# The residual moves into the output projection's sum on TensorE, and ScalarE copies the sum out

## The reference, cut to what matters

```
xn  = layernorm(groupnorm(x)) * ln_w + ln_b          # over 384 channels, per token
xb, z = split(xn @ in_proj_w.T)                       # 768 channels each
xc  = silu(conv1d(xb, 4 taps) + conv_b)
dt, B, C = split(xc @ x_proj_w.T);  dt = softplus(dt @ dt_w.T + dt_b)
h[t] = exp(dt[t] * A) * h[t-1] + dt[t] * xc[t] * B[t] # 768 channels x 16 states
y[t] = sum over states of h[t] * C[t], plus xc * D
x1  = x + (y * silu(z)) @ out_proj_w.T                # the residual and the output projection
```

## Time and profile before

| | |
|---|---|
| median of 3 runs | 7631.88 us (7631.62 to 7632.93) |
| time of the profiled execution | 7631.1 us |
| its span, first to last instruction | 7629.1 us |
| busy over the span | PE 86%, DVE 81%, POOL 70%, ACT 63% |
| mean granted TensorE clock | 0.91 of full speed |
| first layer | about 180 to 5973 us of the span, 32 chunks of 179 to 181 us |
| second layer | the last 1650 us |

### The profile page before, as it was taken

The page is one execution under the profiler, slowest core; times in us unless marked ns, Lnnn a source line. Parts: engine busy times, 40 slices in busy tenths (PEclk is TensorE's granted clock), DMA queues, the critical chain, the costliest instruction groups (busy, mean ns, idle before and its releaser), DMA issues. The chain is left out here.

```text
span 7629.1 us, 100783 instructions
## 1 busy us (share of the span) xinstructions
PE 6579.7 (86%) x33755; PEld 4120.7 (54%) x33755; DVE 6166.0 (81%) x7739; ACT 4784.9 (63%) x8830; POOL 5364.1 (70%) x4339
## 2 busy tenths in 40 slices
PE   4888888888888888888888888888888799999999
PEld 2444444445444444454444444544444577777777
DVE  4999999999999999998999999999999544454444
ACT  2777777777777777777777777777777333333333
POOL 0989899998999999998989999989999200000000
PEclk9898898898898898888988988899888899999999
DMA  4322222222222222332222222222222211111111
GB/s 190 129 92 92 95 94 94 90 92 97 91 91 97 92 91 102 110 111 98 92 92 95 96 92 90 95 95 92 95 93 92 110 51 44 45 51 51 51 51 42
DMA packets 159531, 678.74 MB, mean 89 GB/s; under 512 B 19052, under 2 KB 19180, under 8 KB 124964
## 3 DMA queue, kind: packets, MB, share of 16 engines
q1 hardware_dynamic: 159012, 672.29, 24.2%
HBM read 515.13 MB, written 157.09 MB: 88 GB/s over the span
## 5 line engine op out<-in xcount | busy, mean ns | idle before, releaser
L787 POOL TENSOR_TENSOR dbx<-u,bb 128x512 f32<-128x512 f32 x3072 | 3835.5, 1274 | 175.6 <-DVE p_da L686 172.0
L686 DVE TENSOR_TENSOR_SCAN p_da<-p_da,state_v,dbx 128x512 f32<-128x512 f32 x2112 | 2629.6, 1275 | 180.3 <-ACT p_da L562 180.3
L562 ACT ACTIVATE p_da<-dt,neg_a 128x512 f32<-128x512 f32 x3076 | 2087.6, 688 | 102.3 <-DVE h L693 29.0
L933 PEld LDWEIGHTS p_yt<-ident,hc_v 128*128 128x128 f32 x8448 | 1123.4, 155 | 1416.0 <-issue 775.5
L933 PE MATMUL p_yt<-ident,hc_v 128*128 128x128 f32 x8448 | 1445.6, 301 | 303.3 <-DVE hc_v L702 295.4
L796 POOL TENSOR_TENSOR hc_g<-h,cc 128x512 f32<-128x512 f32 x960 | 1223.0, 1274 | 370.0 <-DVE h L693 366.6
L702 DVE TENSOR_TENSOR hc_v<-cc,p_da 128x512 f32<-128x512 f32 x2112 | 1395.4, 668 | 89.8 <-PE p_yt L933 89.8
L867 PE MATMUL p_g<-xn,win 128*128 128x512 f32 x2376 | 1209.2, 618 | 114.4 <-ACT xc L510 53.2
L693 DVE TENSOR_TENSOR_SCAN h<-p_da,state_g,dbx 128x512 f32<-128x512 f32 x960 | 1219.9, 1271 | 75.9 <-issue 75.3
L568 ACT ACTIVATE state_v<-p_da 128x1 f32<-128x1 f32 x2112 | 353.9, 168 | 1357.4 <-DVE hc_v L702 1348.8
L1296 POOL TENSOR_TENSOR x_low<-axn,x_upper 128x512 fp32r<-128x512 f32 x102 | 135.8, 1359 | 1471.7 <-DVE x_upper L1258 1471.7
(11 more groups left out here) (151 smaller groups left out, 8310.3 us busy)
## 6 DMA issues: line engine op xcount, KB each, us to landing
bb<-bc_spill SPq DMA_DIRECT2D x132, 1024.0 KB, 8.7
cc<-bc_spill SPq DMA_DIRECT2D x132, 1024.0 KB, 7.1
xc_spill<-xc SPq DMA_DIRECT2D x99, 512.0 KB, 2.6
z_spill<-zt SPq DMA_DIRECT2D x99, 512.0 KB, 3.6
xj<-xc_spill SPq DMA_DIRECT2D x193, 256.0 KB, 2.7
zj<-z_spill SPq DMA_DIRECT2D x192, 256.0 KB, 2.7
xs<-in_x SPq DMA_DIRECT2D x34, 768.0 KB, 4.3
axn<-x SPq DMA_DIRECT2D x34, 768.0 KB, 5.8
```

The lines of the kernel that those rows point to most:

```text
L562: nc.scalar.activation(p_da[n % RD][:], dt[:, d % 2, :], ACT.Exp, scale=neg_a[:, d, n:n + 1])\
L686: nc.vector.tensor_tensor_scan(psum, psum, dbx[:, n % RB, :], state_v[:, d, k:k + 1], ALU.mult, ALU.add).then_inc(s_scan, 1)
L787: nc.gpsimd.tensor_tensor(dbx[:, n % RB, :], u[:, d % 2, :], bb[:, n, :], ALU.mult)\
L933: last = nc.tensor.matmul(p_yt[d % 2][:, b * P:(b + 1) * P], product[:, b * P:(b + 1) * P], ident[:], start=False, stop=n == NS - 1, is_tr ...
```

## The change

Three parts. PE begins each output sum with a matmul of the identity and x (`ident`, `back`), for which it waits until x is loaded (`s_rl`). ACT copies the finished sum from PSUM into `back` in its slots 13, 18 and 21 and counts `s_res` (`copy_out`); the additions on DVE are gone. DVE takes the statistics two slots behind `RESIDUAL_AT` (slots 15, 20 and 23) instead of one.

```
+            def copy_out(i, j):
+                act.wait_ge(s_om, i * NJ + j + 1)
+                nc.scalar.activation(back[:, j, :], p_g[G_BANK["out", j]][:], ACT.Copy).then_inc(s_res, 1)
...
                         if SCALE_AT <= g < SCALE_AT + NJ:
                             scale(q, g - SCALE_AT)
+                        if g in RESIDUAL_AT:
+                            copy_out(i, RESIDUAL_AT.index(g))
...
             copy_y(NCH, 0)
+            for j in range(NJ):
+                copy_out(NCH, j)
...
-            def residual(i, j):
-                dve.wait_ge(s_om, i * NJ + j + 1)
-                if j == 0:
-                    dve.wait_ge(s_rl, i * 16 + 16)
-                nc.vector.tensor_tensor(back[:, j, :], back[:, j, :], p_g[G_BANK["out", j]][:], ALU.add).then_inc(s_res, 1)
...
-                        if g in RESIDUAL_AT:
-                            residual(i, RESIDUAL_AT.index(g))
-                        if g - 1 in RESIDUAL_AT:
-                            statistics(i, RESIDUAL_AT.index(g - 1))
+                        if g - 2 in RESIDUAL_AT:
+                            statistics(i, RESIDUAL_AT.index(g - 2))
...
             for j in range(NJ):
-                residual(NCH, j)
                 statistics(NCH, j)
...
+                if t == 0:
+                    pe.wait_ge(s_rl, i * 16 + 16)
+                    nc.tensor.matmul(p_g[G_BANK["out", j]][:], ident[:], back[:, j, :], start=True, stop=False)
                 last = nc.tensor.matmul(p_g[G_BANK["out", j]][:], wout[:, t, j, :], yg[:, t, :],
-                                        start=t == 0, stop=t == ND - 1)
+                                        start=False, stop=t == ND - 1)
```

More of the change, by code:

```diff
@@ L40 @@
 NU = HEADS // 2
+NQ = DIM // P
 TAPS = HALO + 1
```

## The result

The changed kernel takes 7707.2 us (median of 4 runs, 7706.2 to 7709.0) against 7631.8 for the kernel before (4 runs): a ratio of 1.0099, 95% interval 1.0082 to 1.0117. It is 75 us slower. The prediction was 7703, with a range from 7640 to 7742. The profiled execution has a span of 7706.9 us, 77.8 more than before.

The account below looks back on a forecast made before the run. DVE is fullest, but waits between engines in slots 8 to 24 decide. 23 x 1.8 + 9 x 2.5 = 64 us, plus 7.5 in the tail, is 71.5 on 7631.1: 7703 us, range 7640 to 7742.

Parts of the forecast that it names:

- Copy 0: ACT's slot 13: the copy follows Exp, keep_state and a decay, so PE's slot 14 starts 1.38 us later.
- Copy 1: ACT's slot 18: `copy_y` waits for PE's later product, the copy follows, and DVE waits 1.8 us at statistics 1.
- Copy 2: ACT's slot 21: the copy stands behind softplus, DVE waits at statistics 2, slot 24 starts 1.5 us later.
- fast kind: Nine of 32 chunks, whose DVE wait at the residual was 0.15 us or none; forecast loss 2.5 us each.
- slow chunks: 23 of 32 chunks, where DVE waited 1.61 us for PE's sum at the residual; forecast loss 1.8 us each.
- The product's price: Each added identity product on PE costs 0.86 us at the high clock; 1.72 at the low clock kept for the range.
- Slot 22 on PE: First `in_step` waits for the last copy after 3.5 us idle; 0.3 us taken for DVE's product of slot 24.
- What follows in the chunk: From slot 24 on the loss is carried over whole, through DVE's waits for decays behind ACT's softplus and silu.
- Given back later: Rival: denser PE keeps its high clock around slot 33, DVE's waits in slots 37 and 39 shrink; 7648 us, chance 0.12.
- More of the low clock: Rival: gaps ahead of the first and last copies lower PE's clock further, 1.2 us more a chunk; 7741 us, chance 0.15.
- The rival that decides: Test in slot 18: whether `copy_y` finds its sum done, forecast 0.9 us late; if on time, 7629 us, chance 0.08.
- The gain comes through: Rival: sums and copies are always done before DVE and PE ask, saving 95 us but for the tail; 7544 us, chance 0.07.

Follow-up runs that it names:

- e9: Changed kernel plus two unread products (four records) on PE ahead of slot 37's `in_step`, which waits for ACT's copy of z: 7676.9 us, 1.0060.
- e6: Changed kernel with only copy 2 moved ahead of softplus, in slot 20; copy 1 stays behind `copy_y`: 7603.9 us, 0.9966.
- e10: Changed kernel with copy 2 ahead of softplus in slot 20, plus two unread filling products on PE ahead of slot 37's `in_step`: 7667.6 us, 1.0047.
- e12: Changed kernel with the identity product ending each sum only in the layer's last projection, behind the loop: 7700.8 us, 1.0092.
- e5: Changed kernel with only copy 1 moved ahead of `copy_y` in slot 18; copy 2 stays behind softplus: 7663.8 us, 1.0043.
- e4: Changed kernel with DVE taking the statistics in slots 15, 22 and 25; ACT's and PE's order kept: 7615.7 us, 0.9978.

## Why the prediction was right, step by step

The sign and the size came out: 7703 forecast, 7707 measured. Up to slot 24 the loss is where it was put, in ACT's copies with other work ahead of them; behind it the path was another, and the total was right by luck. The steps in the chunk of the earlier trace rows, in us behind `centre` (rows of before less 3082.60, rows of after less 3119.41):

| step | before | predicted | measured |
|---|---|---|---|
| 1 Variance: `normalise` starts | 18.98 | 17.55 | 17.47 |
| 2 Copy 0: PE's slot 14 starts | 17.70 | 19.08 | 18.81 |
| 3 Copy 1: PE's product of slot 15 starts | 26.87 | 29.5 | 29.25 |
| 3 wait at statistics 1 | none | 1.8 | 1.59 |
| 4 Softplus: DVE's product of slot 20 | 33.19 | 33.05 | 32.80 |
| 5 Copy 2: wait at statistics 2 | none | 1.9 | 1.60 |
| 5 scan of slot 24 | 38.52 | 40.03 | 39.77 |
| 6 first `in_step` | 34.60 | 39.55 | 39.27 |

Each time is some 0.25 early against the forecast, and that from step 2 on: 1/std was done at 17.43 for 17.5, copy 0 at 18.76 for 18.9, and PE's matmul began 0.05 behind it for 0.15. The waits named in "What would show it" are all there: the statistics 1.59 and 1.60, `copy_y` 26.0 us in 33 places (0.8 each, forecast 0.9), PE's wait of 2.98 ahead of `in_step` (forecast 3.5), PE's wait for copy 0 (1.3 us in eight chunks of the fast kind, about 0.25 in the others), the chunk of 182.2 (181 to 183), the DMA in the tail. `in_step`'s first record is 4.7 later behind `centre` but 3.6 against slot 14; the forecast's own times give 3.6 too, and its "about 5" holds for `centre` only. Over all chunks the scan of slot 24 is 1.59 later (mean start 39.69 against 38.10), where the steps gave 23 x 1.5 and 9 x 2.2, 1.7 in the mean. By kind it is 1.3 later in the slow chunks (39.8 against 38.5) and 2.1 in the fast ones (39.2 against 37.1). Two slips of the text change nothing: the three chunks without a listed wait at the residual had 0.15 us too, and 0.9 us either way in a chunk would give 7674 to 7731, not 7670 to 7725.

**The product's price.** 0.86 held, not 1.72. The first identity product, right behind slot 8's gap, takes 0.93 from start to start (3124.95 to 3125.88), and the six records behind it 4.43 where the same six took 4.51. The clock falls about as soon behind the gap: in the three us that begin 1.02 behind the first record it is 0.50 (3125.97 to 3128.97), as in the earlier trace rows, and from 3129 on it is 0.99. In the tail 0.86 did not hold: the first identity product takes 1.84 from start to start (6028.68 to 6030.52), at a granted clock of 0.50. The Trainium skill ("TensorE: Matmul & The Clock Gate", Part 1) calls the cold phase a span of time and not a number of matmuls; the trace agrees so far that a product more didn't lengthen it, and doesn't tell the two readings apart, since the number of slow records stayed the same too.

**Slot 22 on PE** lay between its two cases: the four records behind the gap took 2.38 us, 0.4 over the 1.98 of the high clock and 1.0 under the 3.4 of a low clock throughout. The 0.3 that I put on DVE's product of slot 24 isn't there in any chunk; DVE has no wait there.

**"What follows in the chunk"** is the step that failed. I carried the loss at slot 24 over whole. The right total hid a wrong path: +1.6 at slot 24, +1.0 at slot 39, +3.6 at slot 55, +2.2 from slot 71 on. Two of my rivals were both partly there. "Given back later" happened: PE, late and dense, has no gap in slot 35, where it idled 2.6 us before, and DVE's waits for it in slots 37 and 39 shrank (`yg` 38.7 to 9.8 us in all). More was given back in slot 70, where DVE's wait for PE went from 2.24 to 1.07 us. "More of the low clock" happened as well, but in slot 37, a place I hadn't looked at: the gap moved there, ahead of `in_step`, and behind it PE's steps run at the low clock. It reaches DVE less by the silu that I had in mind than directly: of the 2.6 us that the changed kernel takes longer from slot 39 to 55, 1.9 are DVE's wait for PE in slot 41, 0.4 a wait for a decay just before it, and 0.2 the wait behind the silu in slot 45 (2.09 against 1.87 in the mean). ACT's second copy of z waits 2.9 us for the same steps. e9 prices the whole at 1.2 us a chunk by taking it away. That the sum of all this came within 0.3 us a chunk of what I carried was luck: e6 and e10, 0.3 us apart at slot 23, end 64 us apart.

**The tail.** 7.5 forecast: 5.0 for the load and 2.6 for the products, less 0.1. Measured a wait of 5.37, and 9.8 behind the last `centre`, 2.3 of it the last chunk's: 7.5. e12 gives back 6.4, and shows the load apart from the loop.

**The rival that decides.** I wrote that even with copy 1 on time, slot 24 would hang on copy 2 and softplus. e5 and e6 show that: copy 1 moved alone leaves +33 us, copy 2 moved alone -27. But the forecast put that case at 7629, carrying a small lead at slot 24 over whole. e5 has the lead, 1.3 us at slot 39, and loses it behind slot 37's gap: 7664. Here too the step that failed is the one behind slot 24. "The gain comes through" at 7544 isn't reached by any order tried; the best is 7589, with ACT's wait for the sum (32.9 us) and DVE's for the copies (34.9) still there.

**Left open.** Why the clock in e10 falls within 0.5 us of the end of slot 35's gap in 28 of 31 chunks, and in e6 in 16 of 31 only 1.2 to 1.5 us behind it, when all these gaps last 2.23 us. Some tens of us in the experiments' differences hang on it, so a single difference between two orders isn't a price of the moved instruction alone.

## What to carry to other kernels

When work moves from the fullest engine to one with room, price its place in that engine's order, not its length: with 0.6-us copies behind `copy_y` and behind a softplus with two table loads the kernel was 75 us slower, with one of them ahead of the softplus 27 us faster than before, and with the copies left there but their results asked for later (e4) 15 us faster. Follow every wait that ends at the moved instruction through a whole period of the loop, TensorE's gaps too: a gap that one place loses turns up in another, and what hangs on the records behind it decides. Try the identity product that adds a term to a sum at the end of the sum, when the engine is in order and others wait for its next results: here that was worth 72 us in one order and 15 in another. And count no wait as lost time before you have looked at what the engine would wait for next.

## What the runs showed of the hardware

More work on TensorE made the kernel 30 us faster (e9: four records in a gap that was 2.4 us long; the four behind it took 1.98 us instead of 3.21). The same four records cost 64 us in another order (e10).

Two gaps of equal length, 2.23 us, have different outcomes: in e6 the first two records behind it take 1.12 us and only the next ones 1.94, in e10 2.07 and 2.08. The granted clock of PE over the 5.7 us behind each, e6 and then e10 (columns: window and length, PE busy and count, granted clock, DMA share, GB/s):
```profile
3123.30:3129.00 5.70, 5.64 (x16) 0.70 0.00 0
```
```profile
3155.90:3161.60 5.70, 5.70 (x10) 0.50 0.00 0
```
0.50 is the low level, 1.2 GHz, throughout; 0.70 is a mix of both. In the kernel before, a gap of 2.62 us in the same slot has 0.50 for 6.5 us behind it (3140.59 to 3147.09). Within one run the outcome differs from chunk to chunk as well: over the 5.7 us behind the gap of slot 35 the granted clock is 0.50 to 0.55 in 12 of 31 chunks of the kernel before and 0.70 in 18; in e6 0.50 to 0.55 in 10, 0.70 in 16 and 1.00 in 5; in e10 0.50 to 0.55 in 28 and 1.00 in 3. So the length of a gap alone doesn't say at which clock the records right behind it run.
